# Shared groups ahead of the experts, and routed rows added to the output by chained scatter DMAs

## What is computed

```python
x = x + attention(layernorm(x))
xt = layernorm(x).reshape(-1, 256)                     # 4096 tokens
scores = softmax(xt @ gate_w.T)                        # 8 experts
_, idx = top_k(scores + gate_bias, 2)                  # two experts per token
weights = take_along_axis(scores, idx, axis=1)
for e in range(8):
    gate_e = sum(where(idx == e, weights, 0.0), axis=1)
    y = y + gate_e[:, None] * (silu(xt @ w1[e].T) * (xt @ w3[e].T) @ w2[e].T)
z = silu(xt @ sw1.T) * (xt @ sw3.T) @ sw2.T            # the shared experts
out = x + y + z
```

## Time and profile before

| | us |
|---|---|
| median of three runs | 640.19 |
| lowest and highest | 639.12 and 642.98 |
| the profiled execution | 642.74 |
| its span in the trace | 641.0 |
| mean granted TensorE clock | 0.943 of full speed |

### The profile page before, as it was taken

The page is one execution under the profiler, slowest core; times in us unless marked ns, Lnnn a source line. Parts: engine busy times, 40 slices in busy tenths (PEclk is TensorE's granted clock), DMA queues, the critical chain, the costliest instruction groups (busy, mean ns, idle before and its releaser), DMA issues.

```text
span 641.0 us, 11509 instructions
## 1 busy us (share of the span) xinstructions
PE 557.7 (87%) x3464; PEld 482.9 (75%) x3464; DVE 458.7 (72%) x1256; ACT 326.4 (51%) x682; POOL 285.6 (45%) x568
## 2 busy tenths in 40 slices
PE   4869899966988996945999999899999999998975
PEld 2766699966758994535888888688888888887764
DVE  4958999696699746587766753666666666665796
ACT  1547988333798823522545432355555555555321
POOL 4006600120480003305677662267776776676590
PEclk9779799978989997986999999899999999999998
DMA  8998000000000006601222222133333333331994
GB/s 277 335 286 6 1 1 2 2 1 1 1 0 2 1 1 254 239 1 68 83 87 93 76 90 80 38 105 103 108 109 101 105 105 109 101 109 67 298 334 156
DMA packets 57130, 63.04 MB, mean 98 GB/s; under 512 B 14736, under 2 KB 50448, under 8 KB 57072
## 3 DMA queue, kind: packets, MB, share of 16 engines
q1 hardware_dynamic: 49216, 43.75, 23.8%
q0 software_dynamic: 6480, 17.90, 7.9%
q10 hardware_dynamic: 1376, 0.66, 0.4%
HBM read 30.64 MB, written 31.65 MB: 97 GB/s over the span
## 4 chain that ended last, share of the span: by engine, by line
PE 51%; DVE 6%; issue 2%; ACT 1%; another core or an unknown queue 1%; POOL 0%; DVEq 0%; POOLq 0%
PE bank L1254 15%; PE bank L1256 14%; PE bank L1255 14%; PE bank L1377 2%; PE bank L1393 2%; PE bank L1262 1%; PE bank L1306 1%; DVE h_lo L1184 1%; DVE hf L1176 1%; DVE XN L1028 1%; DVE X L1167 1%; PE bank L1279 0%; DVE X L1157 0%; DVE mv L1025 0%
## 5 line engine op out<-in xcount | busy, mean ns | idle before, releaser
L874 POOL DMA_INDIRECT slots_in<-X,slot x64 | 66.8, 1044 | 61.1 <-DVE slot L1141 30.6
L910 POOL DMA_INDIRECT token_out<-YS,to_row x71 | 71.9, 1012 | 49.0 <-DVE back L1221 45.0
L616 PE MATMUL a_bank<-VO,E_hi 128*128 128x258 f32 x272 | 79.5, 292 | 7.9 <-DVE E_lo L519 7.8
L620 PE MATMUL a_bank<-VO,E_lo 128*128 128x258 f32 x272 | 78.9, 290 | 0.0
L618 PE MATMUL a_bank<-VO,E_hi 128*128 128x256 f32 x272 | 78.7, 289 | 0.0
L1210 DVE TENSOR_TENSOR hr<-bank,sr 128x256 f32<-128x256 f32 x71 | 30.2, 425 | 60.9 <-ACT sr L987 60.9
L1254 PE MATMUL bank<-W_hi,XST_hi 128*128 x142 | 62.3, 439 | 0.5 <-DVE XST_lo L1226 0.5
L616 PEld LDWEIGHTS a_bank<-VO,E_hi 128*128 128x128 f32 x272 | 53.7, 197 | 9.0 <-DVE E_lo L519 9.0
L987 ACT ACTIVATE sr<-bank 128x256 f32<-128x256 f32 x71 | 27.3, 385 | 64.6 <-PE bank L1256 62.8
L1256 PE MATMUL bank<-W_hi,XST_lo 128*128 x142 | 57.2, 403 | 0.0
L961 ACT ACTIVATE h_hi<-hf 128x512 fp32r<-128x512 f32 x32 | 20.2, 632 | 71.9 <-DVE hf L1176 62.2
(11 more groups left out here) (239 smaller groups left out, 1711.1 us busy)
## 6 DMA issues: line engine op xcount, KB each, us to landing
XS<-slots_in SPq DMA_DIRECT2D x71, 131.0 KB
slots_in<-blank SPq DMA_DIRECT2D x7, 1179.0 KB, 14.7
YG<-token_out SPq DMA_DIRECT2D x16, 512.0 KB, 8.8
W_raw<-in_wT_dram SPq DMA_DIRECT2D x8, 768.0 KB, 13.7
X<-in_x_dram SPq DMA_DIRECT2D x8, 512.0 KB, 7.9
out_dram<-X SPq DMA_DIRECT2D x32, 128.0 KB, 1.9
token_out<-YS,to_row POOLq DMA_INDIRECT x71, 2.5
slots_in<-blank SPq DMA_DIRECT2D x1, 1048.0 KB, 13.7
```

The costliest lines, as they stand in the source:

```text
L616: pe.matmul(O_ps[Q % 2][j][:, 0:D + 2], E_hi[:, n % NE, cols], VO[:, kt, 0:D + 2], start=(kt == 0), stop=False)
L620: mm = pe.matmul(O_ps[Q % 2][j][:, 0:D + 2], E_lo[:, n % NE, cols], VO[:, kt, 0:D + 2], start=False, stop=(kt == qt))
L874: pool.indirect_dma_start(out=xs, out_offset=bass.IndirectOffsetOnAxis(ap=slot[k][:, t:t + 1], axis=0), in_=X[:, t, :], in_offset=None).th ...
L910: pool.indirect_dma_start(out=ys, out_offset=bass.IndirectOffsetOnAxis(ap=to_row[:, i:i + 1], axis=0), in_=YS[:, i % NYS, :], in_offset=No ...
```

## The change

All eight shared groups are done in stage 3; SP stores each group's finished rows (x plus attention plus shared experts) to the output in one DMA of 512 KB as soon as its sum is ready. There is no token_out and no YG any more, and stage 5 is gone. HOME is the token's row number in the output, and 4096 in empty rows, which the scatter leaves out by its bounds check. POOL's scatter of a slot's results adds them in the DMA to the rows that lie in the output (`compute_op=ALU.add`). Since both choices of a token now have the same destination, POOL waits before each of these scatters until the one before has landed, and before the first until all eight stores have. DVE no longer computes `back`, and POOL one small operation less per slot. The DMA that wrote row numbers to the empty slots during the attention is replaced by a constant in `blank`.

```diff
@@ -53,9 +53,8 @@
     xs = nc.dram_tensor("slots_in", (NSLOT * P, RW), f32, kind="Internal").ap()
-    ys = nc.dram_tensor("token_out", ((TOPK * NT + NSLOT) * P, D), f32, kind="Internal").ap()
+    rows_v = out.rearrange("b s d -> (b s) d")
     xs_p = xs.rearrange("(i p) d -> p i d", p=P)
-    ys_p = ys.rearrange("(n p) d -> p n d", p=P)
     outer = ExitStack()
...
@@ -225,9 +223,6 @@
             sp.wait_ge(s_zero, 128)
-            sp.dma_start(xs_p[:, :, HOME:HOME + 1], no_row[:, :].unsqueeze(2), allow_slow_non_contiguous=True)\
-              .then_inc(s_zero, 16)
-            sp.wait_ge(s_zero, 144)
...
@@ -238,10 +233,9 @@
             pool.memset(blank[:, :], 0.0).then_inc(s_const, 1)
-            pool.iota(no_row[:, :], pattern=[[P, NSLOT]], base=TOPK * NT * P, channel_multiplier=1,
-                      allow_small_or_imprecise_dtypes=True).then_inc(s_const, 1)
-            pool.wait_ge(s_const, 8)
+            pool.wait_ge(s_const, 7)
             pool.memset(blank[:, FIRST:FIRST + 1], -1.0).then_inc(s_const, 1)
+            pool.memset(blank[:, HOME:HOME + 1], float(P * NT)).then_inc(s_const, 1)
             pool.affine_select(out=ident[:, :], in_=ident[:, :], compare_op=ALU.not_equal, fill=1.0, base=0,
...
@@ -791,19 +783,6 @@
         N_XN, N_T, N_XTL = 0, KC * NG, KC * NG + 2 * KC
-        HALF = 6
-
-        def place(G):
-
-            return G % 2 if G < HALF else (G - HALF) % 2
-
-        def group_to_add(n):
-
-            return {2: [0], 3: [1], 4: [2], 5: [3], 6: [4], 7: [5, 6]}.get(n - MC * HALF, [])
-
-        def rows_back(v):
-
-            return 16 * len(range(v, NSLOT, NYS))
...
@@ -817,27 +796,26 @@
                   .then_inc(s_wr, 16)
-            sp.wait_ge(s_T, N_T + KC * HALF)
-
+
+            def residual(G):
+                sp.wait_ge(s_zf, 2 * G + 2)
+                sp.dma_start(out_v[:, G * GT:G * GT + GT, :], X[:, G * GT:G * GT + GT, 0:D]).then_inc(s_out, 16)
+
+            for G in range(NG - 1):
+                residual(G)
+            sp.wait_ge(s_T, N_T + KC * NG)
             for g in range(NG):
...
                 sp.dma_start(XS[:, k, :], xs_p[:, k, :]).then_inc(s_xs[k], 16)
+            residual(NG - 1)
             for i in range(4, NSLOT):
...
                 sp.dma_start(XS[:, i % 4, :], xs_p[:, i, :]).then_inc(s_xs[i % 4], 16)
+            sp.wait_ge(s_out, 16 * NG)
             for v in range(NYS):
-                sp.wait_ge(s_yst[v], rows_back(v))
-            for g in range(NG):
-                for k in range(TOPK):
-                    sp.dma_start(YG[:, g * GT:(g + 1) * GT, k, :],
-                                 ys_p[:, k * NT + g * GT:k * NT + (g + 1) * GT, :]).then_inc(s_yg[g], 16)
-            for g in range(NG):
-                for t in range(g * GT, g * GT + GT):
-                    sp.wait_ge(s_y, t + 1)
-                    sp.dma_start(out_v[:, t, :], X[:, t, 0:D]).then_inc(s_out, 16)
-            sp.wait_ge(s_out, 16 * NT)
+                sp.wait_ge(s_yst[v], 16 * len(range(v, NSLOT, NYS)))
...
@@ -849,7 +827,7 @@
             const(pool.memset(ones_f[:, :], 1.0))
-            const(pool.iota(X[:, :, HOME], pattern=[[P, NT]], base=P * NT, channel_multiplier=1,
+            const(pool.iota(X[:, :, HOME], pattern=[[P, NT]], base=0, channel_multiplier=1,
                             allow_small_or_imprecise_dtypes=True))
...
@@ -890,31 +868,29 @@
                 pool.wait_ge(s_xs[i % 4], 16 * (i // 4) + 16)
-                pool.wait_ge(s_sel, 2 * i + 2)
-                pool.tensor_tensor(home[:, i:i + 1], back[:, i:i + 1], row[:, HOME:HOME + 1], ALU.add).then_inc(s_meta, 1)
-                pool.tensor_tensor(by_weight[:, i:i + 1], is_first[:, i:i + 1], row[:, DW:DW + 1], ALU.mult)\
+                pool.wait_ge(s_sel, i + 1)
+                pool.tensor_copy(to_row[:, i:i + 1], row[:, HOME:HOME + 1]).then_inc(s_mt, 1)
+                pool.tensor_tensor(extra[:, i:i + 1], is_first[:, i:i + 1], row[:, DW:DW + 1], ALU.mult)\
                     .then_inc(s_meta, 1)
-                pool.wait_ge(s_meta, 2 * i + 2)
-                pool.tensor_copy(to_row[:, i:i + 1], home[:, i:i + 1]).then_inc(s_mt, 1)
-                pool.tensor_tensor(by_weight[:, i:i + 1], by_weight[:, i:i + 1], row[:, W1:W1 + 1], ALU.add)\
+                pool.wait_ge(s_meta, i + 1)
+                pool.tensor_tensor(by_weight[:, i:i + 1], extra[:, i:i + 1], row[:, W1:W1 + 1], ALU.add)\
                     .then_inc(s_mt, 1)
...
                 meta_of(i)
+            pool.wait_ge(s_out, 16 * NG)
             for i in range(NSLOT):
...
                 pool.wait_ge(s_ys, i + 3)
-                pool.indirect_dma_start(out=ys, out_offset=bass.IndirectOffsetOnAxis(ap=to_row[:, i:i + 1], axis=0),
-                                        in_=YS[:, i % NYS, :], in_offset=None).then_inc(s_yst[i % NYS], 16)
-            for g in range(NG):
-                pool.wait_ge(s_yg[g], 16 * TOPK)
-                for h in range(0, GT, 2):
-                    tiles = slice(g * GT + h, g * GT + h + 2)
-                    pool.tensor_tensor(YG[:, tiles, 0, :], YG[:, tiles, 0, :], YG[:, tiles, 1, :], ALU.add)\
-                        .then_inc(s_yy, 1)
+                if i > 0:
+                    pool.wait_ge(s_yst[(i - 1) % NYS], 16 * ((i - 1) // NYS) + 16)
+                pool.indirect_dma_start(out=rows_v,
+                                        out_offset=bass.IndirectOffsetOnAxis(ap=to_row[:, i:i + 1], axis=0),
+                                        in_=YS[:, i % NYS, :], in_offset=None, bounds_check=P * NT - 1,
+                                        oob_is_err=False, compute_op=ALU.add).then_inc(s_yst[i % NYS], 16)
...
@@ -1008,10 +984,6 @@
                     output(i, i % 2)
-            group_hi(HALF)
-            for v in range(NYS):
-                act.wait_ge(s_yst[v], rows_back(v))
-            shared(range(HALF, NG))
...
@@ -1148,15 +1120,6 @@
-            def add_routed(g):
-
-                dve.wait_ge(s_zf, 2 * g + 2)
-                for h in range(0, GT, 2):
-                    tiles = slice(g * GT + h, g * GT + h + 2)
-                    dve.wait_ge(s_yy, g * 2 + h // 2 + 1)
-                    dve.tensor_tensor(X[:, tiles, 0:D], X[:, tiles, 0:D], YG[:, tiles, 0, :], ALU.add)\
-                       .then_inc(s_y, 2)
-
             def add_shared(G, z):
...
@@ -1218,8 +1178,6 @@
                                   ALU.is_equal).then_inc(s_sel, 1)
-                dve.tensor_scalar(back[:, i:i + 1], row[:, FIRST:FIRST + 1], which[:, i:i + 1], -float(P * NT),
-                                  ALU.is_equal, ALU.mult).then_inc(s_sel, 1)
...
@@ -1236,14 +1194,6 @@
                     hidden_lo(i + 1, (i + 1) % 2)
-            dve.wait_ge(s_xsT, NSLOT)
-            dve.wait_ge(s_mt, 2 * NSLOT)
-            group_xn(HALF)
-            group_lo(HALF)
-            for v in range(NYS):
-                dve.wait_ge(s_yst[v], rows_back(v))
-            shared(range(HALF, NG))
-            add_routed(NG - 1)
...
@@ -1355,10 +1305,10 @@
             pe.matmul(C_ps[1][:, 0:NT * NX], ones_b[:, :], rhs, start=True, stop=True).then_inc(s_cnt, 1)
-            shared(range(HALF), (0, 1))
+            shared(range(NG), (0, 1))
             pe.wait_ge(s_slot, 3)
             pe.wait_ge(s_wrl, KC * NX)
-            pe.wait_ge(s_zf, 2 * HALF)
+            pe.wait_ge(s_zf, 2 * NG)
...
@@ -1414,9 +1364,6 @@
                     down(i, v, i % 4)
-            group_transpose(HALF)
-            pe.wait_ge(s_ys, NSLOT + 2)
-            shared(range(HALF, NG), ())
...
```

26 lines of the change are left out of this document (10 added, 16 removed).

## The result

| | before | after |
|---|---|---|
| median (us) | 640.43 | 785.16 |
| lowest and highest | 639.12 and 642.98 | 784.90 and 785.39 |
| the profiled execution, its span | 642.74, 641.0 | 785.39, 783.6 |
| mean granted TensorE clock | 0.943 | 0.898 |

The before column has one more run than the three of the first table. The ratio is 1.225, with a 95% interval from 1.222 to 1.229: 22.5% slower. The forecast was 720 us with a range of 652 to 789. The direction holds, and so does the place; the size was 65 us short, and the time is near that of the rival "read, then write, in series" (778).

A forecast was written before the change was run, and what follows sets the result against it. PE bounds the slots before, POOL's chain of waiting scatters after: span = 450.6 + 70 (2.83 + δ) + 2.5 + δ + 0.2 = 721.0 us for δ = 0.98, less 0.8 gives 720 us; range 652 to 789.

The forecast's parts named there:

- read, then write, in series: Rival for the adding scatter: old row read before the write, δ of 1.4 to 2.5, 778 us; chance 0.19.
- The bound: In the slots: PE sets 2.55 us per slot before; after, POOL's chain of 71 waiting scatters does, at 3.81 us.
- What is moved: Two shared groups go ahead of the slots, which begin 35.7 us later, at 439.4; first scatter at 450.6 us.
- The end: Behind the last scatter's start: landing after 2.5 + δ, then 0.2 us to the end of the span.
- δ: What the addition lengthens each results' scatter by: 0.98 us, from 0.38 for bytes and 0.6 for reading the old row.
- the gain on offer: Whole kernel, if the wait on each scatter cost nothing: span 632.9 instead of 641.0 us, only 8 us.
- The period of a plain chain: Results' scatters in the slots, each waiting, without addition: T = 1.01 issue + 1.82 wait = 2.83 us.
- As cheap as a plain one: Rival for the results' chain: δ from −0.26 to 0.1, period 2.57 to 2.93 us, no change in time; chance 0.06.
- Only the bytes are paid: Rival for the adding scatter: old row read beside YS, δ = 0.375 (0.1 to 0.6), 677 us; chance 0.21.
- The chain hides under PE: Rival in the slots: δ below −0.26, period no more than PE's 2.55 us, 632 us; chance 0.08.
- PE's clock falls: Rival in the slots: idle PE drops to clock 0.50 in half the slots, period near 4.5, 771 us; chance 0.04.
- What the profile was to show: Amid the slots: scatters 3.8 us apart, a DMA releasing POOL's wait, PE busy two thirds at clock 1.00.

The follow-up runs named there:

- run 2: The kernel before with one wait more: each results' scatter waits until the one before has landed, without addition or bounds check; 695.13 us, ratio 1.086.
- run 6: The kernel after with two chains: odd slots add to a second tensor, each scatter waits for the one before last; 652.64 us, ratio 1.020.
- run 4: The kernel after with 4096 as every row number, so that the bounds check leaves out all rows of all scatters; 715.07 us, ratio 1.116.
- run 10: The kernel after with POOL's wait for the landing written first and that for ACT's result last; 778.48 us, ratio 1.217.
- run 1: The kernel after without the addition in the results' scatter; the wait and the bounds check stay; 695.52 us, ratio 1.087.
- run 9: The kernel after with each of the 64 plain scatters to the slots also waiting for the one before to land; 839.39 us, measured once.
- run 3: The kernel before with the addition alone, into a zero-filled token_out, without the wait or bounds check; 652.44 us, ratio 1.019.
- run 8: The kernel after with scatters that add only 128 of the 256 columns of each result row; 752.03 us, ratio 1.176.

## Why the prediction was right or wrong

**The bound, right.** The wait puts POOL's scatters in a row, and this row sets the end from the first scatter on; the groups ahead and the tail behind matter little beside it. Runs 2 and 6 show it from both sides: the wait alone on the kernel before costs 55 us, and two chains instead of one bring the time back to 652.6.

**What is moved, right within 3 us.** The slots were to begin at 439.4 us and the first scatter to start at 450.6; they stand at 436.8 and 448.15. No store held up the first scatter: the eighth was issued at 436.9 us, and these stores land after 3.1 us.

**The end, too short by 4.** I gave the end 2.5 + δ + 0.2 = 3.7 us behind the last scatter's start. The span ends 7.5 us behind it, at 783.6, though that scatter has landed after 2.7. Runs 4, 6 and 10, which end on the same scatters, have 7.6 too, and run 1 has 10.4. Nothing in these stretches is busy; what the 5 to 8 us are stays open. Run 1's end is 7.7 us over the 2.7 that I gave a plain scatter, nearly all of the 8 us that I called the gain on offer.

**The period of a plain chain, too short by 0.5: the step that failed first.** "With the issue of a result's scatter, 1.01 us, T = 1.01 + 1.82 = 2.83" took the time after the issue from six waits in the scatters to the slots. Issue and flight carried over; the time from landing to the next start did not: 0.27 us there (run 9), 0.77 to 0.87 at the results (runs 1 and 2). The trace of the kernel before had the right one: its results' scatters start 0.76 us behind ACT's write (run 10), and 2.46 + 0.76 = 3.22 is run 2's period of 3.23. Run 1 measures 3.36 on average for 2.83, times 70 periods: 37 us.

**The addition, too cheap by a quarter: the step that failed next.** δ was forecast as 0.98 and is 4.68 − 3.36 = 1.32, times 70: 24 us. I had put all of it into the flight and left POOL's issue at 1.01, which the prediction names as a term that can fail. It is this term that was missing: the issue went to 1.57, 0.56 of the 1.32 (run 3). The rival "read, then write, in series" had said that POOL might need longer. What is left for the flight is 0.76, less than my 0.98. The empty scatters split it likewise: they land after 2.0 to 2.1 us plain (run 1) and 2.7 adding (run 4), so 0.6 to 0.7 is paid without any row, and the other 0.6 to 0.7 comes with the rows. Of my 0.98 I had 0.38 for the bytes, taking an adding scatter to occupy the DMA engines twice as long as a plain one. By the queue's line it is three times: 12.6% of 783.6 us are 98.7; the 64 scatters to the slots have 0.35 each, as in run 1 (6.9% of 693.3 us over 135), 22.7 in sum; the rest over 71 is 1.07 us. That rival came nearest in time, but its mechanism isn't shown: whether the old row is read ahead of the write or beside it the runs don't say, since the flight goes with the bytes (runs 4 and 8) either way.

The page of the Trainium skill that I weighed against this ("DMA: Bandwidth & Descriptors", the anatomy of one DMA on the gpsimd path) has about 2 us of a DMA as fixed. With this the runs agree: a plain scatter whose rows are all left out lands 2.0 to 2.1 us after its start (run 1), an adding one after 2.7 (run 4). Its rate for the bytes gave 0.30 us for the old rows; the addition measured 1.32, about half of it with the rows, and this decides.

**The sum.** From the forecast's span of 721.0: the first scatter 2.5 earlier, −2.5; the plain period, +37.1; the addition, +24.1; the end, +3.8: 783.6 − 721.0 = 62.6 us. The median lies 1.6 us above the span instead of 0.8 below, and that makes the 65. So the two terms of the period carry the miss, and both were too small.

**The rivals.** "As cheap as a plain one" falls with run 1: its T was at most 2.93, and the plain chain itself has 3.36. "Only the bytes are paid" falls with δ, 1.32 where it had at most 0.6. "The chain hides under PE" has its nearest kin in run 6, where hardly any flight is waited for: 650.9 us in span, 18 us over the 632.9 in span: 17 since POOL's longer issue and what hangs on it set the pace (70 periods of 2.80), 5 at the end, less 3.5 for the earlier start. "PE's clock falls": I forecast a clock of 1.00, and 0.86 was granted amid the slots, against 1.00 before and 1.00 in run 1 from 500 to 600 us, with PE busy 87.7 of 100. So the clock did fall, but it cost next to nothing. Behind the third scatter the chain of work passes through PE at two places, 534 to 541 and 628 to 631 us, and the periods there are 4.72 to 4.87 us. Six periods of 5.1 to 5.95 stand above 4.65 by 5.8 us in sum, without PE: one is a flight of 4.96 us, and in five the chain goes over POOL's small operations, the load of a slot (2.3 to 3.0 us) and DVE. Those small operations and loads I had said would "suffer nothing"; they do wait behind the chain, at little cost. (The prediction's 771 us for this rival should be 769, by its own T of 4.5.)

**What the profile was to show.** The releaser of POOL's wait was to be a DMA. It is one in 21 of 71 lines of the timeline; 39 name ACT. The landing as the last releaser is seen in the chain of work, not in those brackets. PE's busy share was to be two thirds, and it was three quarters at the lower clock.

## What to carry to other kernels

A chain of DMAs, in which each waits for the landing of the one before, costs at each step the flight (counted from the start of the issue) and the restart (from the landing to the next start); set this sum (here 4.65 us) against the pace of the engine that bounds the stage (2.55) before trading an independent destination for it, and count what is on offer in return (here 8 us on paper, nothing in the measurement). An addition and a wait that cost 12 and 55 us alone cost 145 together, since the chain brings to the path what was hidden. A price read from a wait elsewhere in the program held for the flight, not for the restart: read the restart at the same instruction, behind any wait that it has already (0.76 us here), or measure it with one run that has the wait and nothing else.

## What the runs showed of the hardware

- An indirect DMA of 128 rows that adds takes POOL 1.57 us to issue instead of 1.01, writes 144 packets instead of 48, and occupies the 16 DMA engines for 1.07 us instead of 0.35; it lands after 3.8 us instead of 2.5.
- Rows left out by the bounds check are not free: the adding scatter with no row at all still has its 144 packets and takes 1.57 us to issue and 2.7 to land (a plain one 2.0 to 2.1); the 16 DMA engines are occupied for 0.09 us. The check itself adds nothing to be seen (1.01 us with it in run 1).
- Two adding scatters in flight, to different tensors, don't slow each other (landing 3.8 in both cases).
- From a landing to the next scatter's start POOL takes 0.27 us at one place and 0.77 to 0.87 at another; at the latter it takes 0.76 behind a wait for ACT, too. The landing's wait put first instead of last saved 0.08; the rest isn't explained.
- A kernel that ends on an indirect scatter had 5 to 8 us behind its landing in which nothing is busy.
